# The second half of the first x moves to ScalarE's queue, and ScalarE rounds Wu ahead of its first gelu

## The chip, the core and the metric

One Trainium2 chip, one of its cores. The metric is the device time of one execution in microseconds (us), lower is better. Five engines work side by side: PE (TensorE, products), DVE (VectorE), ACT (ScalarE), POOL (GpSimd) and SP (SyncE, which only issues transfers here). Semaphores order them; nothing else does.

## The reference

Each of four batches picks one of three experts (rows of the weight arrays) and runs an adapter on its own x of 512 tokens by 512 features:

```
Wd, bd, Wu, bu, g, b = W_down[e], b_down[e], W_up[e], b_up[e], ln_w[e], ln_b[e]   # e = expert of the batch
h   = gelu(x @ Wd + bd)              # 512x512 @ 512x256, exact gelu
y   = x + (h @ Wu + bu)              # 512x256 @ 256x512
out = (y - mean(y)) / sqrt(var(y) + 1e-5) * g + b       # over the 512 features of each token
```

All of it is float32.

## The kernel before

**Tiling.** A batch's x arrives transposed (features on the 128 partitions) in four blocks k of 128 features by 512 tokens. Two transfers bring it, `load_x(b, 0)` for k = 0, 1 and `load_x(b, 1)` for k = 2, 3, 512 KB each. `load_wd(b)` (516 KB, with the biases), `load_wu(b)` (512 KB) and `load_ln(b)` (512 KB) bring the rest of a batch. All of it stays in buffers of its own, so no load waits for a buffer.

**Precision.** Except for the first half of the first batch, a float32 product is made from three fast ones: a value is split in `hi` (rounded to the fast type) and `lo` (the rest), and hi*hi + hi*lo + lo*hi is summed in PSUM. ACT rounds weights (`hi_wd`, `hi_wu`) and part of x (`hi_x`, x blocks from batch 1's k = 2 on), POOL subtracts to get `lo_wd`, `lo_wu` and `lo_x`. DVE splits the first six x blocks itself (`split_x`: a cast, line 346, and a subtraction, line 348) and the hidden values (`lo_hidden`, line 354). The first 128 columns of the first batch's Wd are used unsplit, in full float32 products (`down_whole`, line 448), so that PE can start on them without waiting for a split.

**PE's order**, written out by hand: `warm_up()` (12 products on an identity matrix, line 441); for each batch the two halves j of the down product (for batch 0 `down_whole(0)`, then `down(0, 1)`, lines 483 to 491); `place_residual` (line 520), which transposes x + bu into the PSUM tile that `up` (lines 535 to 541) then adds to, for four tiles t of 128 tokens. `down_whole` waits for the first half of x and of Wd ahead of k = 0, and for the second halves ahead of k = 2. `up` at t = 0 waits for `hid_hi`, `wu_hi`, `wu_lo` and, ahead of its third product, for `hid_lo`. In batch 1, `place_residual(1, t)` waits until tile t of batch 0 has been normalised (`finish`, line 392, on DVE).

**ACT's order at the start**: issue the transfer of the first half of the first x (line 312), load the gelu table, wait for both halves of the first Wd, round columns 128 to 255 of it (line 316), then `residual(0)` (four instructions, line 293, the third of which waits for the second half of x), `gelu(0, 0)` (two instructions, lines 299 and 301, behind the down product), `hi_wu(0)` (line 285, behind the transfer of Wu), `gelu(0, 1)`, `hi_x(1, 1)` (line 275), `hi_wd(1)` (line 279), `hi_wu(1)`, `residual(1)`.

**DVE's order at the start**: `split_x(0, k)` for k = 0 to 3, `split_x(1, 0)`, `lo_hidden(0, 0)`, `lo_hidden(0, 1)`, `split_x(1, 1)`, then batch 0's statistics (lines 365 to 373), `centre` (line 382) and `finish`.

**POOL's order at the start**: the identity matrix, the low part of the first Wd (line 243), `lo_wu(0, 0)` and `lo_wu(0, 1)` (line 226), `lo_x(1, 2)` and `lo_x(1, 3)` (line 215, behind `hi_x(1, 1)`), `lo_wd(1, 0)`, `lo_wd(1, 1)` (line 221), and the inverse deviations of batch 0 (line 231).

**SP's order at the start**: read batch 0's expert into a register, issue the two halves of the first Wd (lines 179 and 180), `load_x(0, 1)`, `load_wu(0)`, `load_x(1, 0)`, `load_x(1, 1)`; read the three other experts into registers (line 185); then per batch the loads of Wd, Wu and ln, and of x from batch 2 on. Stores follow at the end.

Of the kernel before, what the change touches and what calls it, by code (L numbers as in the profile page):

```python
# [13 lines left out]
DMA = 16  # L14
# [3 lines left out]
def conditional_adapter_kernel(  # L18
# [5 lines left out]
    out: bass.AP,  # L24
):
    B, _, _, HALF, S = x_cols.shape
    KT = 2 * HALF
    H = KT * P
# [15 lines left out]
    with ExitStack() as ctx:  # L44
        def sb(name, shape, dt=F32):
            return ctx.enter_context(nc.sbuf_tensor(name, shape, dt, align_bytes=64))

        def sem(name):
            return ctx.enter_context(nc.semaphore(name))


        x_raw = sb("x_raw", [P, B, KT, S])
# [25 lines left out]
        def raw_wd(b, k0, k1):  # L78
            return w_raw[:, b, k0 * BN:k1 * BN].rearrange("q (k n) -> q k n", n=BN)

        def raw_wu(b, j0, j1):
            return w_raw[:, b, WU0 + j0 * H:WU0 + j1 * H].rearrange("q (j n) -> q j n", n=H)

        def bias_down(b, j):
            return w_raw[:, b, BIAS0 + j:BIAS0 + j + 1]

        def bias_up(b, k):
            return w_raw[:, b, BIAS0 + JT + k:BIAS0 + JT + k + 1]


        x_in = [[sem(f"x_in{b}{c}") for c in range(2)] for b in range(B)]
# [47 lines left out]
        def psum_of_half(half):  # L139
            return LAST % 2 if half == 0 else 1 - LAST % 2  # L140
# [10 lines left out]
        @block.sync  # L151
        def _(sp):
            expert = [sp.value_load(expert_of_batch[0:1, 0:1], min_val=0, max_val=weights.shape[0] - 1)]

            def row_of(b):
                return weights[bass.ds(expert[b], 1), :, :].rearrange("e q n -> (e q) n")

            def load_x(b, c):
                ks = slice(HALF * c, HALF * (c + 1))
                sp.dma_start(x_raw[:, b, ks, :], x_cols[b, c]).then_inc(x_in[b][c], DMA)  # L160

            def load_wd(b):
                sp.dma_start(w_raw[:, b, 0:WD_END], row_of(b)[:, 0:WD_END]).then_inc(wd_in[b], DMA)

            def load_wu(b):
                sp.dma_start(w_raw[:, b, WU0:WROW], row_of(b)[:, WU0:WROW]).then_inc(wu_in[b], DMA)

            def load_ln(b):
                sp.dma_start(ln_gb[:, b, :, :].rearrange("q a h -> q (a h)"),
                             ln_rows[bass.ds(expert[b], 1), :].to_broadcast([P, 2 * H])).then_inc(ln_in[b], DMA)  # L170

            def store(b):
                for c in range(2):
                    ts = slice(2 * c, 2 * c + 2)
                    sp.wait_ge(norm_done, TT * b + 2 * c + 2)
                    sp.dma_start(out_rows[b, :, ts, :], result[:, b % 2, ts, :]).then_inc(stored[b][c], DMA)


            sp.dma_start(w_raw[:, 0, 0:HALF * BN], row_of(0)[:, 0:HALF * BN]).then_inc(first_wd_in[0], DMA)
            sp.dma_start(w_raw[:, 0, HALF * BN:WD_END], row_of(0)[:, HALF * BN:WD_END]).then_inc(first_wd_in[1], DMA)  # L180
            load_x(0, 1)
            load_wu(0)
            load_x(1, 0)
            load_x(1, 1)
            _, others = nc.values_load_multi_w_load_instructions(
                expert_of_batch[0:1, 1:B], engines=(mybir.EngineType.SP,), min_val=0, max_val=weights.shape[0] - 1)
            expert.extend(others)
            for b in range(1, B):
                if b > 1:
                    load_x(b, 0)  # L190
                    load_x(b, 1)
                load_wd(b)
                load_wu(b)
                load_ln(b - 1)
            load_ln(LAST)
            for b in range(LAST):
                store(b)
            for t in range(TT):
                if t == SHARED_T:
                    sp.wait_ge(shifted, 1)  # L200
                else:
                    sp.wait_ge(last_norm_done, LAST_ON_DVE.index(t) + 1)
                sp.dma_start(out_rows[LAST, :, t, :], result[:, LAST % 2, t, :]).then_inc(stored_last[t], DMA)

            for b in range(LAST):
                for c in range(2):
                    sp.wait_ge(stored[b][c], DMA)
            for t in range(TT):
                sp.wait_ge(stored_last[t], DMA)
# [58 lines left out]
        @block.scalar  # L268
        def _(act):
            def hi_x(b, c):  # L270
                p, ks = b % 2, slice(HALF * c, HALF * (c + 1))
                act.wait_ge(x_in[b][c], DMA)
                if b >= 2 and c == 0:
                    act.wait_ge(hid_ps_done, JT * (b - 1))
                nc.scalar.activation(x_hi[:, p, ks, :], x_raw[:, b, ks, :], ACT.Copy).then_inc(x_hi_done, 1)  # L275

            def hi_wd(b):
                act.wait_ge(wd_in[b], DMA)
                nc.scalar.activation(wd_hi[:, b % 2, :, :], raw_wd(b, 0, KT), ACT.Copy).then_inc(wd_hi_done, 1)

            def hi_wu(b):
                act.wait_ge(wu_in[b], DMA)
                if b >= 2:
                    act.wait_ge(y_done, TT * (b - 1))
                nc.scalar.activation(wu_hi[:, b % 2, :, :], raw_wu(b, 0, JT), ACT.Copy).then_inc(wu_hi_done, 1)  # L285

            def residual(b):
                act.wait_ge(wd_in[b], DMA)
                if b >= 2:
                    act.wait_ge(res_placed, TT * (b - 1))  # L290
                for k in range(KT):
                    act.wait_ge(x_in[b][k // HALF], DMA)
                    nc.scalar.activation(x_res[:, b % 2, k, :], x_raw[:, b, k, :], ACT.Identity,  # L293
                                         bias=bias_up(b, k)).then_inc(x_res_done, 1)

            def gelu(b, j):
                p = b % 2
                act.wait_ge(hid_ps_done, JT * b + j + 1)
                nc.scalar.activation(hid_hi[:, p, j, :], hid_ps[:, p, j, :], ACT.Gelu,  # L299
                                     bias=bias_down(b, j)).then_inc(hid_hi_done, 1)  # L300
                nc.scalar.activation(hid_ps[:, p, j, :], hid_ps[:, p, j, :], ACT.Gelu,
                                     bias=bias_down(b, j)).then_inc(hid_done, 1)

            def gelu_half(half, j):
                p, q, tokens = LAST % 2, psum_of_half(half), half_tokens(half)
                act.wait_ge(hid_ps_done, JT * (LAST + half) + j + 1)
                nc.scalar.activation(hid_hi[:, p, j, tokens], hid_ps[:, q, j, 0:S // 2], ACT.Gelu,
                                     bias=bias_down(LAST, j)).then_inc(hid_hi_done, 1)
                nc.scalar.activation(hid_ps[:, q, j, 0:S // 2], hid_ps[:, q, j, 0:S // 2], ACT.Gelu,
                                     bias=bias_down(LAST, j)).then_inc(hid_done, 1)  # L310

            act.dma_start(x_raw[:, 0, 0:HALF, :], x_cols[0, 0]).then_inc(x_in[0][0], DMA)
            nc.scalar.preload_act_table(ACT.Gelu)
            for c in range(2):
                act.wait_ge(first_wd_in[c], DMA)
            nc.scalar.activation(wd_hi[:, 0, :, P:BN], raw_wd(0, 0, KT)[:, :, P:BN],
                                 ACT.Copy).then_inc(first_wd_hi_done, 1)
            residual(0)
            gelu(0, 0)
            hi_wu(0)  # L320
            gelu(0, 1)
            hi_x(1, 1)
            hi_wd(1)
            for b in range(1, B):
                hi_wu(b)
                residual(b)
                if b < LAST:
                    hi_x(b + 1, 0)
                    hi_wd(b + 1)
                    gelu(b, 0)  # L330
                    gelu(b, 1)
                    hi_x(b + 1, 1)
            for half in range(2):
                for j in range(JT):
                    gelu_half(half, j)
            act.wait_ge(rstd_done, TT * LAST + SHARED_T + 1)
            act.wait_ge(centred, TT * LAST + SHARED_T + 1)
            nc.scalar.activation(result[:, LAST % 2, SHARED_T, :], y_ps[:, SHARED_T, :], ACT.Copy,
                                 scale=rstd[:, LAST % 2, SHARED_T:SHARED_T + 1]).then_inc(scaled, 1)
# [266 lines left out]
```

## Time and profile before

| | |
|---|---|
| median of 3 runs | 69.96 us (69.6 to 72.02) |
| the profiled execution, its own time | 69.84 us |
| its span in the trace | 67.6 us |
| PE busy | 57.4 us, 85% of the span |
| DVE busy | 49.4 us, 73% |
| POOL busy | 40.1 us, 59% |
| ACT busy | 34.8 us, 51% |
| read from memory, written | 10.50 MB, 4.19 MB |
| granted TensorE clock | full in every slice up to the last products |

The span runs from the first to the last event of the trace; 2.24 us of the execution's time lie around it. Busy shares are means over the whole span. They don't say which engine is waited for at a given place, so the sections below go by place: by line, and by stretches of time counted from the span's start.

### The profile page before, as it was taken

What the parts mean: (1) busy time and instruction counts of PE and PEld (TensorE: products, weight loads), DVE (VectorE), ACT (ScalarE), POOL (GpSimd) and SP (SyncE); (2) the same over time, 40 slices, a digit from 0 to 9 for tenths busy, and PEclk for the clock granted to TensorE, in tenths of its full rate; (3) what the DMA queues carried; (4) which work ended last, traced back from release to release, by engine and by line L of the source; (5) the groups of instructions that cost most, each with busy time, mean ns of one, the idle gap of its engine ahead of it and who ended that gap; (6) DMA issues with size and microseconds to landing.
All of it is one profiled execution on the core that took longest, in us unless ns stands there. A gap on an engine that the chain in (4) does not pass through costs nothing. (4 is left out here: it accounts for less than half of the span.)

```text
span 67.6 us, 975 instructions
## 1 busy us (share of the span) xinstructions
PE 57.4 (85%) x300; PEld 47.9 (71%) x300; DVE 49.4 (73%) x95; ACT 34.8 (51%) x51; POOL 40.1 (59%) x43
## 2 busy tenths in 40 slices
PE   0999907999999999999999999999999999991000
PEld 0999204689888888888888879888999898870000
DVE  0066007771999999977999985499999979999900
ACT  3400917579999746499990529994045404040000
POOL 4000420029899929999998999999389003227300
PEclk9999999999999999999999999999999999999955
DMA  0929999499999999999980034600000653400650
GB/s 0 308 45 321 237 344 412 189 237 408 293 405 421 413 376 419 394 425 417 422 334 24 5 155 191 274 0 0 10 0 0 264 211 145 155 5 0 257 205 4
DMA packets 4468, 14.75 MB, mean 218 GB/s; under 512 B 496, under 2 KB 496, under 8 KB 4464
## 3 DMA queue, kind: packets, MB, share of 16 engines
q1 hardware_dynamic: 4320, 14.17, 55.8%
q10 hardware_dynamic: 144, 0.52, 2.3%
q8 instruction: 2, 0.03, 0.2%
q14 instruction: 2, 0.02, 0.1%
HBM read 10.50 MB, written 4.19 MB: 217 GB/s over the span
## 5 line engine op out<-in xcount | busy, mean ns | idle before, releaser
L226 POOL TENSOR_TENSOR wu_lo<-w_raw,wu_hi 128x512 fp32r<-128x512 f32 x8 | 10.2, 1290 | 5.9 <-ACT wu_hi L285 5.9
L535 PE MATMUL y_ps<-wu_hi,hid_hi 128*128 128x512 f32 x32 | 13.4, 418 | 0.0
L215 POOL TENSOR_TENSOR x_lo<-x_raw,x_hi 128x512 fp32r<-128x512 f32 x10 | 13.2, 1341 | 0.2 <-ACT x_hi L275 0.2
L541 PE MATMUL y_ps<-wu_hi,hid_lo 128*128 128x512 f32 x32 | 12.6, 394 | 0.0
L537 PE MATMUL y_ps<-wu_lo,hid_hi 128*128 128x512 f32 x32 | 12.5, 392 | 0.0
L365 DVE BATCH_NORM_STATS2 stats<-y_ps 128x6 f32<-128x512 f32 x16 | 10.9, 691 | 2.3 <-PE y_ps L541 2.2
L231 POOL TENSOR_TENSOR rstd<-var_eps,minus_half 128x2 f32<-128x2 f32 (+1 forms) x10 | 6.4, 638 | 10.4 <-DVE var_eps L373 10.4
L382 DVE SCALAR_TENSOR_TENSOR y_ps<-y_ps,mean_var,ln_gb 128x512 f32<-128x512 f32 x16 | 11.5, 750 | 0.0
L293 ACT ACTIVATE x_res<-x_raw,w_raw 128x512 f32<-128x512 f32 x16 | 10.3, 717 | 1.8 <-DMA x_raw<-x_cols 1.8
L392 DVE SCALAR_TENSOR_TENSOR result<-y_ps,rstd,ln_gb 128x512 f32<-128x512 f32 x15 | 10.8, 744 | 0.3
L346 DVE CAST x_hi<-x_raw 128x512 fp32r<-128x512 f32 x6 | 2.6, 433 | 8.6 <-DMA x_raw<-x_cols 8.6
L520 PE MATMUL y_ps<-ident,x_res 128*128 128x128 f32 x64 | 8.6, 272 | 0.0
L520 PEld LDWEIGHTS y_ps<-ident,x_res 128*128 128x128 f32 x64 | 7.6, 140 | 1.2
L483 PE MATMUL hid_ps<-x_hi,wd_hi 128*128 128x512 f32 x20 | 8.2, 410 | 0.0
L299 ACT ACTIVATE hid_hi<-hid_ps,w_raw 128x512 fp32r<-128x512 f32 x6 | 4.1, 691 | 7.6 <-PE hid_ps L491 6.9
L491 PE MATMUL hid_ps<-x_hi,wd_lo 128*128 128x512 f32 x20 | 7.8, 390 | 0.0
L487 PE MATMUL hid_ps<-x_lo,wd_hi 128*128 128x512 f32 x20 | 7.8, 389 | 0.0
L221 POOL TENSOR_TENSOR wd_lo<-w_raw,wd_hi 128x512 fp32r<-128x512 f32 x6 | 7.7, 1295 | 0.0
L541 PEld LDWEIGHTS y_ps<-wu_hi,hid_lo 128*128 128x128 f32 x32 | 6.0, 187 | 1.3
L537 PEld LDWEIGHTS y_ps<-wu_lo,hid_hi 128*128 128x128 f32 x32 | 6.1, 189 | 0.9
L535 PEld LDWEIGHTS y_ps<-wu_hi,hid_hi 128*128 128x128 f32 x32 | 6.0, 189 | 0.9
L441 PE MATMUL y_ps<-ident 128*128 128x128 f32 x24 | 5.2, 410 | 1.5 <-POOL ident L237 1.5
(35 smaller groups left out, 87.4 us busy)
## 6 DMA issues: line engine op xcount, KB each, us to landing
x_raw<-x_cols SPq DMA_DIRECT2D x7, 512.0 KB, 7.5
out<-result SPq DMA_DIRECT2D x6, 512.0 KB, 2.6
w_raw<-weights SPq DMA_DIRECT2D x4, 512.0 KB, 7.8
ln_gb<-ln_rows SPq DMA_DIRECT2D x4, 512.0 KB, 12.2
w_raw<-weights SPq DMA_DIRECT2D x3, 516.0 KB, 8.2
out<-result SPq DMA_DIRECT2D x4, 256.0 KB, 2.4
x_raw<-x_cols ACTq DMA_DIRECT2D x1, 512.0 KB, 3.2
w_raw<-weights SPq DMA_DIRECT2D x1, 260.0 KB, 2.7
```

Of the source, the lines that this page charges most:

```text
L215: nc.gpsimd.tensor_tensor(x_lo[:, b % 2, k, :], x_raw[:, b, k, :], x_hi[:, b % 2, k, :].bitcast(F32), ALU.subtract).then_inc(x_lo_done, 1)
L226: nc.gpsimd.tensor_tensor(wu_lo[:, b % 2, j, :], raw_wu(b, j, j + 1)[:, 0, :], wu_hi[:, b % 2, j, :].bitcast(F32), ALU.subtract).then_inc( ...
L293: nc.scalar.activation(x_res[:, b % 2, k, :], x_raw[:, b, k, :], ACT.Identity, bias=bias_up(b, k)).then_inc(x_res_done, 1)
L365: nc.vector.bn_stats(stats[:, b % 2, t, :], y_ps[:, t, :]).then_inc(stats_done, 1)
L382: nc.vector.scalar_tensor_tensor(out=y_ps[:, t, :], in0=y_ps[:, t, :], scalar=mean_var[:, p, t, 0:1], in1=ln_gb[:, b, 0, :], op0=ALU.subtract,
L392: nc.vector.scalar_tensor_tensor(out=result[:, p, t, :], in0=y_ps[:, t, :], scalar=rstd[:, p, t:t + 1], in1=ln_gb[:, b, 1, :], op0=ALU.mul ...
L483: nc.tensor.matmul(hid_ps[:, p, j, :], wd_hi[:, p, k, cols], x_hi[:, p, k, :], start=(k == 0), stop=False)
L487: nc.tensor.matmul(hid_ps[:, p, j, :], wd_hi[:, p, k, cols], x_lo[:, p, k, :], start=False, stop=False)
L520: last = nc.tensor.matmul(y_ps[:, t, k * P:(k + 1) * P], x_res[:, b % 2, k, t * P:(t + 1) * P], ident[:], start=(k == 0), stop=False, is_t ...
L535: nc.tensor.matmul(y_ps[:, t, :], hid_hi[:, p, j, rows], wu_hi[:, p, j, :], start=False, stop=False, skip_group_check=True)
L537: nc.tensor.matmul(y_ps[:, t, :], hid_hi[:, p, j, rows], wu_lo[:, p, j, :], start=False, stop=False, skip_group_check=True)
L541: last = nc.tensor.matmul(y_ps[:, t, :], hid_lo[:, p, j, rows], wu_hi[:, p, j, :], start=False, stop=(j == JT - 1), skip_group_check=True)
```

## The change

Two edits. The transfer of the second half of the first x is no longer SP's third transfer; ACT issues it right behind that of the first half, ahead of its table load. And ACT rounds the first Wu before the first gelu, where it did so after. All waits stay where they were in the helpers, and the buffers, sizes and arithmetic are the same.

```diff
@@ SP (block.sync)
             sp.dma_start(w_raw[:, 0, 0:HALF * BN], row_of(0)[:, 0:HALF * BN]).then_inc(first_wd_in[0], DMA)
             sp.dma_start(w_raw[:, 0, HALF * BN:WD_END], row_of(0)[:, HALF * BN:WD_END]).then_inc(first_wd_in[1], DMA)
-            load_x(0, 1)
             load_wu(0)
             load_x(1, 0)
             load_x(1, 1)
@@ ACT (block.scalar)
-            act.dma_start(x_raw[:, 0, 0:HALF, :], x_cols[0, 0]).then_inc(x_in[0][0], DMA)
+            for c in range(2):
+                act.dma_start(x_raw[:, 0, HALF * c:HALF * (c + 1), :], x_cols[0, c]).then_inc(x_in[0][c], DMA)
             nc.scalar.preload_act_table(ACT.Gelu)
             for c in range(2):
                 act.wait_ge(first_wd_in[c], DMA)
             nc.scalar.activation(wd_hi[:, 0, :, P:BN], raw_wd(0, 0, KT)[:, :, P:BN],
                                  ACT.Copy).then_inc(first_wd_hi_done, 1)
             residual(0)
+            hi_wu(0)
             gelu(0, 0)
-            hi_wu(0)
             gelu(0, 1)
```

## Rows read from the trace of the kernel before

**Rows 1.** The page: busy us, share of the span and instructions of each engine.
```profile
PE 57.4 (85%) x300; PEld 47.9 (71%) x300; DVE 49.4 (73%) x95; ACT 34.8 (51%) x51; POOL 40.1 (59%) x43
```

**Rows 2.** Who waited for whom: engine, line, releaser: total us, times, longest.
```profile
PE hid_ps L448 <- DMA x_raw<-x_cols: 2.1, 1, 2.1
```

**Rows 3.** Stretches: length, busy of the engines, granted clock, DMA share, GB/s.
```profile
3.50:4.00 0.50, 0.50 (x4) 0.50 (x4) 0.02 (x1) 0.00 (x0) 0.00 (x0) 1.00 0.00 0
...
8.42:10.54 2.12, 0.01 (x2) 0.00 (x1) 0.02 (x1) 0.36 (x2) 0.53 (x1) 1.00 0.95 357
...
12.50:60.00 47.50, 47.50 (x266) 40.76 (x265) 41.20 (x80) 29.98 (x45) 35.75 (x32) 1.00 0.60 231
```

**Rows 4.** Timeline of PE's weight loads, start and length in us, around the wait.
```profile
6.43 0.30 PEld L448 LDWEIGHTS hid_ps<-x_raw,w_raw 128*128 128x128 f32 x2
...
7.41 0.19 PEld L448 LDWEIGHTS hid_ps<-x_raw,w_raw 128*128 128x128 f32 x1 [0.24 <-issue]
...
10.54 0.30 PEld L448 LDWEIGHTS hid_ps<-x_raw,w_raw 128*128 128x128 f32 x2 [2.94 <-DMA x_raw<-x_cols]
...
11.93 0.19 PEld L483 LDWEIGHTS hid_ps<-x_hi,wd_hi 128*128 128x128 f32 x1 [0.24 <-issue]
```

**Rows 5.** Timeline of ACT, up to the residual of batch 1.
```profile
0.74 0.37 ACTq L312 DMA_DIRECT2D x_raw<-x_cols  x1
...
6.90 0.63 ACT L316 ACTIVATE wd_hi<-w_raw 128x512 fp32r<-128x512 f32 x1 [4.48 <-DMA w_raw<-weights]
...
13.72 1.06 ACT L285 ACTIVATE wu_hi<-w_raw 128x1024 fp32r<-128x1024 f32 x1
15.31 0.69 ACT L299 ACTIVATE hid_hi<-hid_ps,w_raw 128x512 fp32r<-128x512 f32 x1 [0.53 <-PE hid_ps L491]
...
19.31 2.56 ACT L293 ACTIVATE x_res<-x_raw,w_raw 128x512 f32<-128x512 f32 x4
```

**Rows 6.** Timeline of SP: transfers issued (line 160 x, 166 Wu, 163 Wd, 169 ln).
```profile
4.50 0.43 SPq L160 DMA_DIRECT2D x_raw<-x_cols  x1
5.11 0.33 SPq L166 DMA_DIRECT2D w_raw<-weights  x1
...
12.56 0.35 SPq L163 DMA_DIRECT2D w_raw<-weights  x1
...
13.62 0.33 SPq L169 DMA_DIRECT2D ln_gb<-ln_rows  x1
```

**Rows 7.** DMA view of issues at 0.74, 5.11, 12.56, 13.62: KB, us to landing.
```profile
x_raw<-x_cols ACTq DMA_DIRECT2D x1, 512.0 KB, 3.2
...
w_raw<-weights SPq DMA_DIRECT2D x1, 512.0 KB, 6.7
...
w_raw<-weights SPq DMA_DIRECT2D x1, 516.0 KB, 3.6
...
ln_gb<-ln_rows SPq DMA_DIRECT2D x1, 512.0 KB, 5.7
```

**Rows 8.** Timelines of DVE and POOL where they touch the same stretch.
```profile
13.05 0.43 DVE L346 CAST x_hi<-x_raw 128x512 fp32r<-128x512 f32 x1 [0.31 <-DMA x_raw<-x_cols]
...
17.69 1.76 DVE L348 TENSOR_TENSOR x_lo<-x_raw,x_hi 128x512 fp32r<-128x512 f32 x1
...
20.99 0.90 DVE L373 TENSOR_SCALAR var_eps<-mean_var 128x2 f32<-128x2 f32 x1
...
17.60 1.30 POOL L215 TENSOR_TENSOR x_lo<-x_raw,x_hi 128x512 fp32r<-128x512 f32 x1 [0.22 <-ACT x_hi L275]
...
18.86 1.75 POOL L215 TENSOR_TENSOR x_lo<-x_raw,x_hi 128x512 fp32r<-128x512 f32 x1
```

**Rows 9.** Timelines of PE and DVE at places where PE needs what DVE made.
```profile
17.32 0.40 PE L541 MATMUL y_ps<-wu_hi,hid_lo 128*128 128x512 f32 x1
...
27.78 1.03 PE L520 MATMUL y_ps<-ident,x_res 128*128 128x128 f32 x8
...
26.11 1.40 DVE L392 SCALAR_TENSOR_TENSOR result<-y_ps,rstd,ln_gb 128x512 f32<-128x512 f32 x2
```

## The prediction

> **What bounds the kernel now.** I read the page's busy shares first: PE is the busiest engine with 57.4 of 67.6 us [rows 1]. Then the list of waits for PE alone: after its start it waited once, 2.1 us for a transfer of x [rows 2]. The stretches place it: from 8.42 to 10.54 us PE is idle at full granted clock, and from 12.50 to 60.00 it is busy 47.5 us of 47.5 [rows 3]. So behind this wait nothing that DVE, ACT or POOL do holds PE, and DVE's last normalisations hang on PE's last products. What PE gains at 10.54 us reaches the end, as long as none of its suppliers is now late.
>
> The wait is for the second half of the first x. SP issued it at 4.50 us and it landed at 10.54, 6.0 us later [rows 4, 6]. The first half, alone on ACT's queue from 0.74 us, took 3.2 us and landed at 3.9 [rows 5, 7]. Behind it the DMA engines have nothing: their share is 0.00 from 3.50 to 4.00 us [rows 3].
>
> **Edit 1, the transfer.** Removed: one issue of 0.43 us on SP [rows 6]. Added: one of 0.37 to 0.43 us on ACT, ahead of its table load; ACT's next work starts at 6.90 us, after 4.48 us of idling [rows 5], so this costs nothing while the first Wd comes no sooner. When does the second half land? At best at 0.7 us behind the first, at worst a full 3.2 us behind it, 7.1 us [rows 7]. I take about 5.3, near the lower end because the engines stand idle there. PE needs it at 7.8, so both ends do.
>
> What PE gains: its four weight loads of k = 0, 1 start at 6.43 to 7.41 us; those of k = 2, 3 start at 10.54, and the fifth load behind that is `down(0, 1)`'s at 11.93 [rows 4]. The first burst's fourth load is 0.98 behind its first, the second burst's fifth 1.39 behind its first, so loads follow by 0.41 to 0.43. Without the wait `down(0, 1)` begins five steps behind 7.41, at 9.5 us, and that is 2.4 us earlier. The wait of 2.1 us alone [rows 2] is the lower bound; it leaves out the restart. I take 2.4.
>
> Who must keep up with a PE that is 2.4 us early:
> - DVE splits k = 2, 3 from about 6.2 us on instead of 10.5, done well before 9.5. The cover is the early landing.
> - The gelu of j = 1 waits only for PE (0.53 us at 15.31) and starts at 12.9. ACT's residual needs no second wait: it follows the rounding of Wd (ends 7.53) and takes 2.56 as in batch 1, so ACT is free at 10.1 [rows 5].
> - Everything that starts from that gelu moves with it: `hi_x(1, 1)`, POOL's x at 17.60, DVE's statistics [rows 8].
> - The later transfers don't move by 2.4: SP still reads three experts into registers and issues Wd(1) at 12.56 and ln at 13.62, now at most 0.6 us earlier (4.50 to 5.11, one issue less) [rows 6]. Wd(1) lands at 16.2, now about 15.7 [rows 7]; ACT asks at 12.9 + 1.4 (two gelus at 0.69) + 1.06, 15.4 [rows 5], and waits 0.3. POOL subtracts it only after its x, at 20.6 less 2.4 = 18.2 [rows 8]. ln lands at 19.3, now 18.8 [rows 7]; DVE's `centre` begins behind the variance at 21.9 less 2.4 = 19.5 [rows 8]. Cost: nothing, with 0.7 us to spare.
> - `place_residual(1, 1)`, the fifth of eight transposes from 27.78 us, begins at 28.3; DVE's second `finish` ends at 27.5 [rows 9]. DVE may fall 0.8 us behind the new schedule before PE feels it.
>
> **Edit 2, Wu ahead of the gelu.** It moves one rounding of 1.06 us [rows 5] and puts a wait for Wu ahead of `gelu(0, 0)`. Behind the waiting instruction stand both gelus, `hi_x(1, 1)` and `hi_wd(1)`. Wu now takes the place that x had in SP's queue. Bounds for its landing: 10.5 us, what x needed there, and 7.8, at 4.6 + 3.2, the pace of the undisturbed first half [rows 4, 6, 7]. ACT is free at 10.1. With 10.5, Wu is rounded at 11.6 and the first gelu pair ends at 13.0, the second asks at 12.9: a cost of 0.1. With anything under 10.1 there is none. POOL's low Wu is then ready at about 14.1, and `up` needs it past 14.6. I take nothing. If Wu came only at 11.8, as before [rows 7], see the third rival.
>
> **Sum.** 69.84 (profiled execution) - 2.4 + 0 = 67.4 us. The median of the runs is 0.12 above that execution, so I say 67.6, 3.4% less.
>
> **Rivals.**
>
> *Port (POOL holds DVE up).* Before, DVE's `split_x(1, 0)` at 13.05 us lay ahead of POOL's work on Wu. Now both come together. The trace shows what that costs: DVE's subtraction at 17.69 took 1.76 us against POOL's from 17.60 to 18.90, then POOL's next took 1.75 in place of 1.30; the tiny addition at 20.99 took 0.90 [rows 8]. They take turns. With Wu at 10.5, POOL starts on it at 11.6; x(1, 0), now in the place in which Wu landed at 11.8, comes 0.2 us too late to go first. If the cast waits too: cast 12.9 to 13.3, POOL to 14.6, DVE's subtraction to 15.2, `lo_hidden(0, 0)` to 15.8. PE needs that at 17.32 - 2.4 = 14.9 [rows 9]: 0.9 us lost, 0.4 if Wu lands at 10.0. Time: 67.9 to 68.5, say 68.2. Against it: x lands a little sooner and the cast goes first, or the cast isn't held; then DVE is done in time. No row of before shows a cast held by POOL. The Trainium skill (SBUF — State Buffer, Who interferes with whom) says that a cast can take the port that DVE shares with GpSimd, that whoever comes first keeps it for its whole instruction, and that the other blocks. By that rule the cast is held as well, and the sum is the 68.2. The durations of the two subtractions agree with it.
>
> *Wu late.* Wu lands at 11.8 us after all. Then it is rounded at 12.9, the second gelu starts at 14.2 instead of 12.9, and DVE and POOL are 1.3 us behind where 0.8 is free; with a turn lost to POOL besides, 0.5 to 1.2 us. Time: 67.9 to 68.7. For it: Wu did land then. Against it: 512 KB less are ahead of it.
>
> *No gain from the queue.* The second half lands hardly sooner, or pushes Wd back by as much. The Trainium skill (DMA: Bandwidth & Descriptors, Issuing engines are not separate DMA queues) says that all issuers' transfers share the same 16 engines, and that a second issuer saves only its time to issue. By that rule alone, only 0.43 us would be won and the time would be 69.4. The row speaks against applying it here: the engines are idle from 3.50 us [rows 3], and this issue comes 3 us earlier, ahead of the read of the expert that Wd has to wait for. Time 69.0 to 69.8.
>
> *Slower: Wd pushed back past the gain.* The second half of x lies across Wd's transfers, both queues share the engines, and PE's first real product waits. Its place is the load at 6.43 us [rows 4]. The price is at most what crowding did to x itself, 6.0 - 3.2 = 2.8 us [rows 4, 6, 7], on top of a warm-up that ends when Wd lands; it decides once Wd's first half comes after 6.4 + 2.4 = 8.8 us. With 2.8 the start is 9.2 and the time 69.84 - 2.4 + 2.8 = 70.2 us. Against it: 1 us of empty engines ahead of Wd.
>
> **Chances.** Forecast 0.52, port 0.27, Wu late 0.08, no gain 0.07, slower 0.06. Within 2% is about what a measurement of this kernel can't tell from no change, and its edge is 68.56 us. Faster by over 2%: forecast, nearly all of port, half of Wu late, 0.81. Slower by over 2% (71.36) needs more than the priced 70.2: 0.03. Within: 0.16. The range from 67.0 (0.3 us of luck with restarts and the 0.6 us earlier loads) to 68.8 takes in the first three cases, 0.87 less their edges.
>
> **What would show it.** Right: PE's wait for x is gone and the first product of `down(0, 1)` starts near 9.5 us; PE busy without a break behind it; the second half of x on DVE (its third cast) at 6.2; ACT's Wu rounding between 10.0 and 11.6. Port: `lo_hidden(0, 0)` ends after 15 us, a cast or subtraction of `split_x(1, 0)` takes over 1 us, and PE waits for `hid_lo` ahead of its third `up` product. Wu late: ACT's rounding of Wu starts after 11 us, released by a transfer. Slower: ACT's first rounding, now at 6.90, starts after 8. I am wrong altogether if PE shows a new wait of over 1 us further on, most likely in batch 1, for a transfer that SP issues no earlier than before.

## The result, and the profile after

The changed kernel takes 68.11 us (median of 4 runs, 67.71 to 68.77) against 69.78 us for the kernel before: ratio 0.9755, 95% interval 0.971 to 0.9799. The forecast was 67.6 us in a range of 67.0 to 68.8. The profiled execution, the fastest of the four, took 67.71 us with a span of 65.8 us, 2.1 and 1.8 us less than before. The ratios and intervals here leave out every run more than 1.5% above the fastest of its kernel, and as the profiled runs of `wu_only`, `quarter`, `both_quarters` and `clear_x_only` were such, only single waits, landings and instructions are read from those.

PE's only wait behind its start is gone. This is the whole list of PE's waits after; before, it had the line of [rows 2] as well:

```profile
PE y_ps L441 <- POOL ident L236: 1.5, 1, 1.5
```

PE's weight loads after, to be laid beside [rows 4] (start us, length, line, tile):

```profile
6.96 0.30 PEld L448 LDWEIGHTS hid_ps<-x_raw,w_raw 128*128 128x128 f32 x2 [0.30 <-issue]
...
8.36 0.19 PEld L448 LDWEIGHTS hid_ps<-x_raw,w_raw 128*128 128x128 f32 x1 [0.24 <-issue]
...
10.07 0.19 PEld L483 LDWEIGHTS hid_ps<-x_hi,wd_hi 128*128 128x128 f32 x1 [0.24 <-issue]
```

The loads of k = 2, 3 follow those of k = 0, 1 at the pace of 0.43 us. But the first of them starts at 6.96 us where it was 6.43, so `down(0, 1)` begins at 10.07, 1.86 us earlier and not 2.4. The reason stands on ACT and in the DMA view. ACT's timeline after (beside [rows 5]):

```profile
0.74 0.87 ACTq L312 DMA_DIRECT2D x_raw<-x_cols  x2
...
7.86 0.63 ACT L316 ACTIVATE wd_hi<-w_raw 128x512 fp32r<-128x512 f32 x1 [4.93 <-DMA w_raw<-weights]
8.40 2.54 ACT L292 ACTIVATE x_res<-x_raw,w_raw 128x512 f32<-128x512 f32 x4
10.85 1.05 ACT L284 ACTIVATE wu_hi<-w_raw 128x1024 fp32r<-128x1024 f32 x1
```

Both halves of x are issued by 1.6 us and the residual runs its four blocks in one piece. But both halves of Wd were in only at 7.86 us, 0.96 later than before, with issue times within 0.05 us of those before. The DMA view of the issues at 3.55 and 4.14 us (KB, us to landing; both took 2.7 before):

```profile
w_raw<-weights SPq DMA_DIRECT2D x1, 256.0 KB, 3.3
...
w_raw<-weights SPq DMA_DIRECT2D x1, 260.0 KB, 3.6
```

The stretches show what was on the engines then (length, busy us of PE, PEld, DVE, ACT, POOL, granted clock, DMA share, GB/s):

```profile
3.50:4.00 0.50, 0.50 (x4) 0.50 (x4) 0.07 (x1) 0.00 (x0) 0.00 (x0) 1.00 1.03 410
4.00:4.50 0.50, 0.50 (x5) 0.50 (x4) 0.47 (x2) 0.00 (x0) 0.00 (x0) 1.00 0.84 344
```

From 3.50 to 4.00 us, empty before [rows 3], the engines now move 410 GB/s. That is x: Wd was only issued at 3.55, and the second half of x landed at about 6.2 us (the DMA view gives 3.2 us for ACT's first transfer and 4.1 as the median of its two, so 5.0 for the second, issued at 1.1). So x and Wd were under way side by side.

**A second execution.** The kernel was run and profiled again (68.04 us, span 66.1), and about as much is lost in another place. PE's loads and its first late product in that execution:

```profile
6.29 0.30 PEld L448 LDWEIGHTS hid_ps<-x_raw,w_raw 128*128 128x128 f32 x2
...
9.40 0.19 PEld L483 LDWEIGHTS hid_ps<-x_hi,wd_hi 128*128 128x128 f32 x1 [0.24 <-issue]
```

```profile
15.76 0.50 PE L541 MATMUL y_ps<-wu_hi,hid_lo 128*128 128x512 f32 x1 [0.82 <-DVE hid_lo L354]
```

Here Wd took as long to land as before the change, PE began `down(0, 1)` at 9.40, 2.5 us earlier, and gave 0.82 back waiting for `hid_lo`. DVE and POOL in that stretch show why:

```profile
11.91 1.51 DVE L346 CAST x_hi<-x_raw 128x512 fp32r<-128x512 f32 x1 [2.45 <-DMA x_raw<-x_cols]
13.46 1.65 DVE L348 TENSOR_TENSOR x_lo<-x_raw,x_hi 128x512 fp32r<-128x512 f32 x1
15.03 1.27 DVE L354 TENSOR_TENSOR hid_lo<-hid_ps,hid_hi 128x512 fp32r<-128x512 f32 x2
```

```profile
11.85 2.71 POOL L225 TENSOR_TENSOR wu_lo<-w_raw,wu_hi 128x512 fp32r<-128x512 f32 x2 [2.94 <-ACT wu_hi L284]
```

POOL began on Wu at 11.85, 0.06 us ahead of DVE's cast. The cast took 1.51 us in place of 0.43, the subtraction 1.65 in place of 0.69, and `lo_hidden(0, 0)` lay behind both. In the first execution x(1, 0) had landed at 11.1 and the cast went first. DVE there:

```profile
11.17 0.43 DVE L346 CAST x_hi<-x_raw 128x512 fp32r<-128x512 f32 x1 [2.71 <-DMA x_raw<-x_cols]
11.63 0.69 DVE L348 TENSOR_TENSOR x_lo<-x_raw,x_hi 128x512 fp32r<-128x512 f32 x1
13.04 0.69 DVE L354 TENSOR_TENSOR hid_lo<-hid_ps,hid_hi 128x512 fp32r<-128x512 f32 x1 [0.71 <-ACT hid_ps L300]
```

### The profile page after: what moved, and what is told of

Its sections match the earlier page's. It is cut to its first block and busy times, and to the rows that moved or that the text cites. A ratio compares the mean times of both kernels' runs of the same rounds, so it can differ in the third digit from the quotient of the medians.

```text
span 65.8 us, 975 instructions
## 1 busy us (share of the span) xinstructions
PE 57.7 (88%) x300; PEld 48.1 (73%) x300; DVE 49.6 (75%) x95; ACT 34.8 (53%) x51; POOL 40.3 (61%) x43
## 5 line engine op out<-in xcount | busy, mean ns | idle before, releaser
L214 POOL TENSOR_TENSOR x_lo<-x_raw,x_hi 128x512 fp32r<-128x512 f32 x10 | 13.2, 1346 | 1.0 <-ACT x_hi L274 1.0
L230 POOL TENSOR_TENSOR rstd<-var_eps,minus_half 128x2 f32<-128x2 f32 (+1 forms) x10 | 6.4, 639 | 10.5 <-DVE var_eps L373 10.5
```

What stands on the lines that cost most here:

```text
L214: nc.gpsimd.tensor_tensor(x_lo[:, b % 2, k, :], x_raw[:, b, k, :], x_hi[:, b % 2, k, :].bitcast(F32), ALU.subtract).then_inc(x_lo_done, 1)
```

## The experiments

Ratios are to the kernel before on the same chip, with 95% intervals. Each kernel has one profile, so a wait read from it is that of one execution. Each kernel is the changed one with the diff shown, unless it says otherwise.

### again: the changed kernel unchanged

> The changed kernel once more, so that its start is seen twice. Crowding theory: the second half of x still streams when the first Wd begins, so Wd's first half lands at about 6.9 us, not 6.2, in this run as well, and PE's first real product starts at 6.9 to 7.0. Chance theory: the 0.5 us later start was a scatter of one execution; it is 6.5 to 6.6 here. Time on both 67.3 to 68.3 us, ratio 0.970 to 0.980.

0.9765 (0.9714 to 0.9815), median 68.12 us. The time is as expected, and the chance theory held for the start: Wd's first half took 2.6 us to land here, as before the change, and 2.6 to 2.7 us in the single profiles of `x_only`, `x10_late`, `clear` and `clear_x_only`. The 3.3 of the first execution isn't a fixed price; what makes it come and go is open.

### x_only: edit 1 alone

```diff
             residual(0)
-            hi_wu(0)
             gelu(0, 0)
+            hi_wu(0)
             gelu(0, 1)
```

> Only the transfer moves; the rounding of Wu stays behind the first gelu. My theory: edit 1 is the whole gain, and the time is that of the changed kernel within 0.2 us (ratio 0.973 to 0.980): ACT is then at the first gelu at 10.9 us, rounds Wu at about 12.2 to 13.3, and up needs its low part only past 15. Rival: the rounding before the gelu is worth something of its own, since POOL would start on Wu at 13.3 instead of 12.0, the low part of j = 1 would be ready at 15.9 against a need at 16.5, and POOL's later work (x of batch 1 from 15.7) slips by 0.2 to 0.4 us: ratio 0.978 to 0.985.

0.9674 (0.9608 to 0.974), median 67.7 us. Edit 1 carries the whole gain; the rival that the early rounding helps fell. That the kernel without edit 2 is faster isn't shown: its six runs scatter from 67.21 to 69.25 us and the intervals overlap. Its profile shows how edit 2 can do harm. x(1, 0) landed about when it did in `again` (11.81 against 11.91 us), but POOL, behind the later rounding, wasn't at Wu yet. DVE, then POOL:

```profile
11.81 0.43 DVE L346 CAST x_hi<-x_raw 128x512 fp32r<-128x512 f32 x1 [3.57 <-DMA x_raw<-x_cols]
12.28 1.80 DVE L348 TENSOR_TENSOR x_lo<-x_raw,x_hi 128x512 fp32r<-128x512 f32 x1
...
12.26 2.97 POOL L225 TENSOR_TENSOR wu_lo<-w_raw,wu_hi 128x512 fp32r<-128x512 f32 x2 [2.88 <-ACT wu_hi L284]
```

Only the subtraction is held, and PE doesn't wait for `hid_lo` in batch 0. The profiled time is no better (68.07 us), for a reason in batch 1 that the section on the prediction shows.

### wu_only: the kernel before with edit 2 alone

```diff
             residual(0)
-            gelu(0, 0)
             hi_wu(0)
+            gelu(0, 0)
```

> Only the rounding moves; the second half of x stays SP's third transfer. My theory: nothing, ratio 0.997 to 1.003. Wu lands at 11.8 us, is rounded by 12.9, the first gelu starts 0.4 us later than before (13.0 for 12.56) and the second is still released by PE at 15.3. Rival: the late first gelu holds up lo_hidden and PE, 0.3 to 0.5 us slower, ratio 1.004 to 1.007.

0.9999 (0.9964 to 1.0035), median 69.69 us. As expected: nothing. In its profile the cast of x(1, 0), at 13.20 us, is held (1.50 us), where in [rows 8] it took 0.43: with edit 2, POOL is at Wu from 13.13 us on, without it from 14.85.

### more_ahead: a third transfer ahead of Wd

```diff
             for c in range(2):
                 act.dma_start(... x_cols[0, c]).then_inc(x_in[0][c], DMA)
+            act.dma_start(x_raw[:, 1, 0:HALF, :], x_cols[1, 0]).then_inc(x_in[1][0], DMA)
...
             load_wu(0)
-            load_x(1, 0)
             load_x(1, 1)
```

> ACT issues a third transfer of 512 KB (the first half of batch 1's x) behind the two of the first x; SP no longer does. Crowding theory: what is ahead of Wd or beside it on the engines delays it. 512 KB more at 400 GB/s are 1.3 us: Wd's first half lands at about 7.5 to 8.2 us, PE's first product at 7.6 to 8.3, and the time is 0.6 to 1.3 us above the changed kernel (ratio 0.984 to 0.995). Rival: the two queues are served in turn, so a longer queue on ACT costs Wd no more than the 0.5 us seen; start 6.9 to 7.1, ratio 0.973 to 0.980.

0.9865 (0.9811 to 0.9919), median 68.81 us. Crowding is shown. Wd's first half, issued at 3.53 us, took this long (DMA view), and PE waited for it (waits of PE):

```profile
w_raw<-weights SPq DMA_DIRECT2D x1, 256.0 KB, 4.6
```

```profile
PE hid_ps L448 <- DMA w_raw<-weights: 1.5, 1, 1.5
```

Its first real load came at 8.21 us and it had no other wait: x(1, 0) was there early, DVE split it at 8.33 to 9.47, long before POOL turned to Wu. So 512 KB more cost Wd 1.3 to 2.0 us against the two profiles of the changed kernel, and they remove that meeting of DVE and POOL.

### quarter: only k = 2 ahead of Wd

```diff
-            for c in range(2):
-                act.dma_start(x_raw[:, 0, HALF * c:HALF * (c + 1), :], x_cols[0, c]).then_inc(x_in[0][c], DMA)
+            act.dma_start(x_raw[:, 0, 0:HALF, :], x_cols[0, 0]).then_inc(x_in[0][0], DMA)
+            act.dma_start(x_raw[:, 0, HALF:HALF + 1, :], x_cols[0, 1][:, 0:1, :]).then_inc(x_in[0][1], DMA)
...
+            sp.dma_start(x_raw[:, 0, HALF + 1:KT, :], x_cols[0, 1][:, 1:HALF, :]).then_inc(x3_in, DMA)
             load_wu(0)
```

(PE, ACT and DVE wait for `x3_in` ahead of k = 3 of batch 0.)

> Only 256 KB (k = 2) go ahead of Wd on ACT's queue; k = 3 is SP's third transfer, with a semaphore of its own. Crowding theory: 768 KB ahead of Wd end by about 4 us, so Wd lands as before the change (6.2 us) and PE starts at 6.5. k = 3, needed at about 9.1, lands between 7.7 and 9.5: ratio 0.966 to 0.976, up to 0.5 us better than the changed kernel. Rival: k = 3 behind Wd is as late as the whole half was (10 us or more), PE waits 1 us for it, ratio 0.980 to 0.990.

0.9895 (0.985 to 0.994), median 69.06 us. The rival held in this profile: 256 KB behind Wd are nearly as late as 512 were. PE's waits:

```profile
PE hid_ps L452 <- DMA x_raw<-x_cols: 0.9, 1, 0.9
```

k = 3 was in at 9.85 us, needed at about 8.7. My hope for a better cut of x fell.

### wd_quarter and both_quarters: a smaller first piece of Wd

```diff
-            sp.dma_start(w_raw[:, 0, 0:HALF * BN], row_of(0)[:, 0:HALF * BN]).then_inc(first_wd_in[0], DMA)
-            sp.dma_start(w_raw[:, 0, HALF * BN:WD_END], row_of(0)[:, HALF * BN:WD_END]).then_inc(first_wd_in[1], DMA)
+            sp.dma_start(w_raw[:, 0, 0:BN], row_of(0)[:, 0:BN]).then_inc(first_wd_in[0], DMA)
+            sp.dma_start(w_raw[:, 0, BN:WD_END], row_of(0)[:, BN:WD_END]).then_inc(first_wd_in[1], DMA)
```

(PE waits for the second ahead of k = 1.) The second kernel has the diff of `quarter` as well.

> The changed kernel with Wd's first transfer holding only k = 0 (128 KB) and the second the rest (388 KB). If PE's start hangs on how much of Wd must land, it comes 0.2 to 0.4 us sooner (6.6 to 6.8), k = 1 waits for the second transfer at about 7.7, needed at 7.6: gain 0 to 0.3 us on the changed kernel. Rival: the landing hangs on the slowest engine and what of x it still holds, not on Wd's size; the start stays at 6.9 and k = 1 now waits too, 0.1 to 0.3 us slower than the changed kernel.

> Both of the two edits before together. If each saves what it should, PE starts at 6.45 (the warm-up's end) and nothing is left for the second edit: the time of the kernel with only k = 2 ahead, within 0.2 us. If k = 1 waits for the larger second part of Wd, 0.2 to 0.4 us slower than that kernel.

`wd_quarter`: 0.9706 (0.9652 to 0.976), median 67.51 us, the lowest median here, but its interval overlaps that of the changed kernel. The small piece landed 2.2 us after its issue, and PE's weight load for k = 1 then stood idle 0.48 us for the large one, where such a load stands idle 0.24 without a wait. `both_quarters`: median 68.83 us against 69.75 for before, without a ratio (one of its six runs is left by the rule above), and nothing is concluded beyond that it isn't the best. In its profile the same 256 KB of k = 3 landed after 3.7 us, at 8.1, and PE didn't wait for them, so the 5.4 us of `quarter` aren't a fixed price either.

### x10_late: DVE's work on x(1, 0) put on top of POOL's

```diff
-            load_x(1, 0)
             load_x(1, 1)
+            load_x(1, 0)
```

> The changed kernel, with SP's load of the second half of batch 1's x ahead of the first half, so that DVE's cast and subtraction for k = 0 of batch 1 are asked for while POOL works on Wu (12.0 to 14.7 us). The first half then lands at 12 to 12.5. Port rival (POOL holds the cast as well): the cast ends at 13.3 to 13.8, the subtraction past 15, lo_hidden(0, 0) at about 16, PE waits 0.5 to 0.9 us for it: ratio 0.982 to 0.990. Other theory (only the subtraction is held): the cast takes 0.43 at once, lo_hidden ends before 15.2, the time is that of the changed kernel.

0.9866 (0.9805 to 0.9926), median 68.4 us. That is 1% above `again` by the ratio and 0.4% by the median, and the two intervals touch, so only the sign is as the port theory has it; its profile ends like that of `again` (PE's last product at 59.33 and 59.29 us). x(1, 0) landed at 13.2 us, in the middle of POOL's second subtraction (11.19 + 2.52, so 12.4 to 13.7). DVE:

```profile
13.19 0.80 DVE L346 CAST x_hi<-x_raw 128x512 fp32r<-128x512 f32 x1 [4.89 <-DMA x_raw<-x_cols]
14.03 0.69 DVE L348 TENSOR_TENSOR x_lo<-x_raw,x_hi 128x512 fp32r<-128x512 f32 x1
```

The cast is held, as the port theory says, though only until POOL is through, and the subtraction then finds POOL idle. PE waited 0.37 us for `hid_lo`, below the 0.5 to 0.9 expected.

### clear and its two relatives: DVE's order

```diff
-            split_x(1, 0)
-            for j in range(JT):
-                lo_hidden(0, j)
+            lo_hidden(0, 0)
+            split_x(1, 0)
+            lo_hidden(0, 1)
             split_x(1, 1)
```

> The changed kernel with one step moved on DVE: lo_hidden(0, 0) ahead of split_x(1, 0). Port theory: PE's wait of 0.8 us for hid_lo in the second execution of the changed kernel came from a cast and a subtraction of split_x(1, 0) held by POOL (1.51 and 1.65 us) with lo_hidden(0, 0) behind them. Here lo_hidden(0, 0) starts when its gelu is done (12.8 to 13.1 us), the held cast and subtraction come behind it, and PE has no wait over 0.2 us for hid_lo: 0.2 to 0.7 us better than the changed kernel, ratio 0.966 to 0.974. Rival: the held work only moves, lo_hidden(0, 1) or batch 0's statistics are late by as much and PE waits at up j = 1 or at the residual of batch 1: time of the changed kernel, ratio 0.974 to 0.980.

0.9745 (0.9713 to 0.9777), median 68.07 us: the changed kernel's time. PE's wait for `hid_lo` at 15 us is gone, and the rival held: the held work only moved. PE and DVE in its profile, in batch 1:

```profile
25.85 1.29 PE L520 MATMUL y_ps<-ident,x_res 128*128 128x128 f32 x8 [0.50 <-DVE result L392]
```

```profile
13.08 1.12 DVE L346 CAST x_hi<-x_raw 128x512 fp32r<-128x512 f32 x1
...
15.45 1.14 DVE L346 CAST x_hi<-x_raw 128x512 fp32r<-128x512 f32 x1
16.62 1.67 DVE L348 TENSOR_TENSOR x_lo<-x_raw,x_hi 128x512 fp32r<-128x512 f32 x1
...
24.96 1.40 DVE L392 SCALAR_TENSOR_TENSOR result<-y_ps,rstd,ln_gb 128x512 f32<-128x512 f32 x2
```

Three of the four operations that split x for batch 1 were held, the statistics started at 18.21 us, and PE waited 0.50 us for batch 0's normalised tile, a place that had 0.8 us to spare before [rows 9]. At 29.22 us it waited once more, for DVE's `hid_lo` of batch 1.

> As the kernel with the moved DVE step, but with Wu rounded behind the first gelu as before the change. Edit 2 worthless theory: within 0.25 us of the other. Rival (edit 2 does harm, since it starts POOL on Wu at 11.9 instead of 12.3 and puts the gelu behind Wu's landing): 0.2 to 0.4 us faster than the other, ratio 0.962 to 0.970. Rival (edit 2 helps POOL): 0.2 to 0.4 us slower.

0.9643 (0.9599 to 0.9687), median 67.91 us, runs from 66.96 to 69.03. By the ratio, which stands on three of the six runs, the rival that edit 2 does harm held; by the medians of all six (67.91 against 68.07) it is worthless. With the pair `x_only` and `again` (67.7 against 68.12) the sign is the same twice, the size stays open.

> The moved DVE step together with Wd's first transfer cut to k = 0 (128 KB). If the start of PE and the turn lost to POOL are separate losses, this keeps both gains: PE starts at 6.1 to 6.4 us, waits for no hid_lo, ratio 0.962 to 0.970 and the fastest here. Rival: they overlap, time of the kernel with the small first Wd (0.9706) within 0.2 us.

0.9822 (0.9781 to 0.9864), median 68.54 us. Both my theories missed: it is slower than either edit alone. In its profile the first piece of Wd landed by 5.6 us, but the second, 388 KB, took 3.6 us and PE's weight load for k = 1 stood idle 1.03 us for it; then PE waited 0.50 us for DVE's normalised tile. In two executions of the same two pieces of Wd (3.3 and 3.6 us for the second) that load thus stood idle 0.48 and 1.03 us.

### sp_first: x issued by SP ahead of its read of the expert

```diff
+            sp.dma_start(x_raw[:, 0, HALF:KT, :], x_cols[0, 1]).then_inc(x_in[0][1], DMA)
             expert = [sp.value_load(expert_of_batch[0:1, 0:1], ...)]
```

(ACT issues only the first half.)

> The second half of x is issued by SP, ahead of its read of the expert, instead of by ACT behind the first half. It costs SP 0.43 us ahead of the read, so Wd is issued at about 3.95 us instead of 3.5. If Wd's landing follows its issue by 2.6 to 2.7 us, PE starts at 6.6 to 6.8 and the time is that of the changed kernel to 0.3 us slower. Rival: with both queues at work from 0.8 us on, x is in sooner and Wd, behind it on SP's own queue, lands when it did: no difference.

1.0009 (0.9975 to 1.0043), median 69.62 us: the whole gain is gone, more than either theory said. SP issued Wd at 4.76 us, 1.2 later, where one issue is 0.43. PE started at 7.46, released by Wd, and later waited for `hid_lo`:

```profile
7.46 3.67 PE L448 MATMUL hid_ps<-x_raw,w_raw 128*128 128x512 f32 x8 [1.18 <-DMA w_raw<-weights]
...
16.79 0.50 PE L541 MATMUL y_ps<-wu_hi,hid_lo 128*128 128x512 f32 x1 [0.68 <-DVE hid_lo L354]
```

The first half of x, now beside the second, landed late too, at 5.8 us instead of 3.9, but PE's start hung on Wd and not on it. So this variant speaks for putting the early issue on a queue that doesn't have to issue Wd as well. Why one issue puts off the next by 1.2 us is open.

## Why the prediction was right, point by point

**What bounds.** Half right. PE's one wait was the price of the order of the loads, and it is gone. But I wrote that what PE gains there reaches the end, and part of it doesn't. How much earlier than before each thing happens (us; in brackets when it happened before):

| | first execution | second (`again`) | `x_only` |
|---|---|---|---|
| weight load of `down(0, 1)` (11.93) | 1.86 | 2.53 | 2.59 |
| `place_residual(1, 0)` (27.78) | 1.85 | 1.47 | 2.18 |
| PE's last product (60.65) | 1.68 | 1.36 | 1.33 |
| end of the span (67.6) | 1.8 | 1.5 | 1.5 |
| the execution's time (69.84) | 2.13 | 1.80 | 1.77 |

**The gain of 2.4 us.** Right for the start: `down(0, 1)` began 2.5 to 2.6 us earlier where Wd landed in time, in `again`, `x_only`, `x10_late`, `clear` and `clear_x_only`, and 1.9 earlier in the first profile. PE kept 1.3 to 1.7 of it.

**"PE starts at 6.43".** The first mis-sized term. I took Wd's landing as unchanged and kept the crowding only as a rival of up to 2.8 us. It was 0.5 us at PE in the first profile and nothing in the second; `more_ahead` shows that it grows with what lies ahead of Wd. The second half of x itself landed at about 6.2 and 5.4 us; I had taken 5.3.

**"I take nothing" for DVE and POOL.** The second. The port rival, priced at 0.9 us for a Wu landing at 10.5, is what the second execution shows almost to the tenth: Wu rounded from 10.71, cast ending at 13.42 (I had 13.3), `lo_hidden(0, 0)` at about 15.7 (15.8), PE's wait 0.82 (0.9), time 68.04 us (68.2). The Trainium skill (SBUF — State Buffer, Who interferes with whom) was right for the cast as well, which no row of before showed: 1.51 us in `again`, 0.80 in `x10_late`, 1.12 in `clear`, each ending about 0.3 us behind POOL's instruction. In the first profile the cast won by 0.8 us and nothing was lost there.

**"DVE may fall 0.8 us behind".** The third, and the one that caps the gain. I measured DVE's spare time at the normalised tile. The next place was tighter. In batch 1 DVE normalises two tiles, makes `hid_lo` for j = 0, normalises two more and makes `hid_lo` for j = 1; the third product of `up(1, 0, 1)` needs the last of these. Before, DVE was through with it at 30.03 us and PE's load came at 30.26, 0.2 us later:

```profile
29.34 0.69 DVE L354 TENSOR_TENSOR hid_lo<-hid_ps,hid_hi 128x512 fp32r<-128x512 f32 x1
...
30.26 0.19 PEld L541 LDWEIGHTS y_ps<-wu_hi,hid_lo 128*128 128x128 f32 x1
```

The same load in the first execution, in `again` and in `x_only`:

```profile
28.71 0.19 PEld L541 LDWEIGHTS y_ps<-wu_hi,hid_lo 128*128 128x128 f32 x1 [0.35 <-DVE hid_lo L354]
```

```profile
29.01 0.19 PEld L541 LDWEIGHTS y_ps<-wu_hi,hid_lo 128*128 128x128 f32 x1 [0.26 <-DVE hid_lo L354]
```

```profile
29.05 0.19 PEld L541 LDWEIGHTS y_ps<-wu_hi,hid_lo 128*128 128x128 f32 x1 [0.69 <-DVE hid_lo L354]
```

DVE had ended at 28.66, 28.95 and 29.00, and from each of these loads PE's last product is 30.26 to 30.28 us away. The load waits for DVE also in the profiles of `x10_late`, `clear`, `clear_x_only` and `clear_wd_quarter`; it doesn't in `wd_quarter`, which has the lowest median. Batch 0's statistics and all that DVE does from them to this subtraction took 10.66 us before (from 19.37 on) and 10.65 in `again` (from 18.30 on), without a wait. So a product that PE does early in batch 0 is worth nothing at the end unless DVE's statistics start as much earlier, and an operation that POOL holds up ahead of them costs about the same wherever it stands in DVE's order. That is why `clear` missed: its statistics started at 18.21 us, those of `again` at 18.30. PE's own list of waits doesn't name this place in the first two executions, since a load can stand idle while the product ahead of it still runs.

**The sum.** The forecast of 67.6 takes 2.4 us off at PE and nothing elsewhere. PE kept 0.7 to 1.1 less in these three profiles, and 0.4 us came back behind PE's last product, where I had forecast nothing. Of this, 0.3 us lies outside the span: time less span is 1.88 to 1.97 us in the ten runs of the changed kernel and 2.16 to 2.27 in the 52 of the kernel before that were measured beside the experiments. It is 2.11 and more also in `wu_only`, `more_ahead`, `quarter`, `both_quarters` and `sp_first`, and at most 2.02 in the others. No run here says why. So it is partly luck that the point was only 0.5 us low: two misses have opposite signs. One loss or another was there in each of these executions, and I had given them chances as separate cases instead of a place in the sum.

**Edit 2.** Right within what was measured: worth nothing (0.9999 alone). I missed that it may do a little harm, by bringing POOL to Wu before the cast.

**The later transfers.** Wrong in part. I let them come up to 0.6 us earlier with the issue that SP is rid of, and left 0.7 us to spare at DVE's `centre`. SP issued Wd(1) at 12.50 us after and 12.56 before. ACT waited 0.35 us for Wd(1) and 0.23 for Wu(1), without cost to PE. But ln landed at about 20.0 us (issued at 13.56, 6.4 to landing), when DVE was through with the variance at 20.03, and in `x_only`, where SP's read ended 0.4 us later, DVE waited for it:

```profile
20.38 1.42 DVE L382 SCALAR_TENSOR_TENSOR y_ps<-y_ps,mean_var,ln_gb 128x512 f32<-128x512 f32 x2 [0.63 <-DMA ln_gb<-ln_rows]
```

And ACT waited 1.51 us for Wd(2) in the first execution, where it was 0.50 before; its gelu for batch 1 stands behind that, and DVE behind the gelu:

```profile
26.06 0.69 DVE L354 TENSOR_TENSOR hid_lo<-hid_ps,hid_hi 128x512 fp32r<-128x512 f32 x1 [0.28 <-ACT hid_ps L300]
```

Both delays lie on DVE's way to the load at 28.71 and 29.05 us.

**The DMA rule.** The Trainium skill's rule (DMA: Bandwidth & Descriptors, Issuing engines are not separate DMA queues), read alone, would have given 69.4 us; the measured 68.11 is below that, because the move was to an earlier time, not only to another issuer. The same rule agrees with `more_ahead` and the first profile: what ACT's queue still holds, SP's transfer pays for.

## What to carry to other kernels

Look for idle DMA time ahead of the first address that must be read, and put there what needs no address; what is still under way when the addressed load begins can cost it: 256 KB of Wd took 2.6 to 3.3 us behind 1 MB of x and 4.6 behind 1.5 MB, against 2.7 behind 512 KB. When an engine is freed by 2 us, check each supplier by place: here a DVE operation and a POOL operation that had never met came to within 0.1 us of each other, and which went first decided 0.8 us there. Ask at every later place too how much the second busiest engine has to spare: PE was busy without a break from 12.50 to 60.00 us before, and yet DVE was only 0.2 us ahead of it at one load, so of 2.5 us won at the start 1.3 to 1.7 were kept. Moving the held work behind the urgent one didn't help, since it still lay on DVE's way to that load.

## What the runs showed of the hardware

- One kernel's executions differ by which of two engines' instructions comes first: 11.17 against 11.91 us for a landing, 0.43 against 1.51 us for the same cast.
- A 128x512 subtraction of DVE on two SBUF inputs takes 0.69 us alone and 1.65 to 1.82 us beside POOL's; POOL's own, 1.27 to 1.30 alone, took 1.51 at 11.97 us in the first execution, beside DVE's at 11.63.
- From SP's last issue ahead of its read of three experts to its issue of Wd(1) lie 5.4 to 6.9 us, and the read doesn't follow what SP issued before it: Wd(1) was issued at 12.50, 11.84, 12.88 and 12.80 us in `after`, `again`, `x_only` and `clear`, and at 10.82 in `more_ahead`, which left one issue less ahead of it. The cause is open.
- A transfer of 256 KB behind Wd took 5.4 us in `quarter` (issued at 4.40) and 3.7 in `both_quarters` (issued at 4.38), one of 512 KB in the same place 6.0.
